# Wide attention: the causal mask written to the scores as four 64x64 tiles instead of two full matmuls

## The reference, cut to what matters

```python
qh = (q @ w_q.T).reshape(b, n, H, D_K).transpose(0, 2, 1, 3)
...
scores = jnp.einsum('bhid,bhjd->bhij', qh, kh) / math.sqrt(D_K)
causal = jnp.tril(jnp.ones((n, n), dtype=bool))
scores = jnp.where(causal[None, None], scores, -jnp.inf)
attn = jax.nn.softmax(scores, axis=-1)
```

## Time and profile before

| | us |
|---|---|
| median of 3 runs | 1951.07 |
| lowest and highest run | 1949.83, 1951.59 |
| profiled execution, its own time | 1948.23 |
| its span, first to last instruction | 1946.2 |
| wide attention in it, first to last mask matmul (L1750) | 353.6 to 800.4 |
| TensorE busy over the whole span | 1779.9 (91%) |
| L1750 within it: 128 matmuls, 379 ns median each | about 33 us of 447 |

### The profile page before, as it was taken

The page is one execution under the profiler, slowest core; times in us unless marked ns, Lnnn a source line. Parts: engine busy times, 40 slices in busy tenths (PEclk is TensorE's granted clock), DMA queues, the critical chain, the costliest instruction groups (busy, mean ns, idle before and its releaser), DMA issues. The chain is left out here.

```text
span 1946.2 us, 43912 instructions
## 1 busy us (share of the span) xinstructions
PE 1779.9 (91%) x16273; PEld 1149.1 (59%) x16273; DVE 1115.4 (57%) x2416; ACT 861.5 (44%) x2151; POOL 613.5 (32%) x1047
## 2 busy tenths in 40 slices
PE   5999878999999999769889999979999989997797
PEld 3555453778778778557763444436777754554343
DVE  4677667566666665561554555552222246776886
ACT  4455425455555555425452333334333344543232
POOL 2667318222222222200103544400000006763440
PEclk9999969999999999869998999978999998999898
DMA  4000040000000000101010000000000010000001
GB/s 108 2 3 3 27 118 6 6 5 7 7 4 7 7 7 2 44 0 44 1 45 1 2 2 2 2 1 0 1 0 0 0 44 2 3 3 2 0 0 43
DMA packets 47708, 27.17 MB, mean 14 GB/s; under 512 B 10928, under 2 KB 44592, under 8 KB 47536
## 3 DMA queue, kind: packets, MB, share of 16 engines
q1 hardware_dynamic: 42800, 24.64, 4.5%
q10 hardware_dynamic: 4736, 0.15, 0.1%
HBM read 22.69 MB, written 2.10 MB: 13 GB/s over the span
## 5 line engine op out<-in xcount | busy, mean ns | idle before, releaser
L708 DVE TENSOR_REDUCE neg_max<-scores 128x8 f32<-128x1024 f32 x192 | 234.8, 1225 | 162.4 <-PE scores L523 66.8
L1708 POOL TENSOR_TENSOR probs<-probs,inverse 128x512 f32<-128x512 f32 x128 | 133.3, 1041 | 337.6 <-DVE inverse L1908 337.6
L651 ACT ACTIVATE probs<-turned 128x1024 f32<-128x1024 f32 x128 | 131.1, 1024 | 224.0 <-PE turned L538 224.0
L493 PE MATMUL scores<-k_diag,q_all 32*128 32x512 f32 x768 | 221.9, 663 | 2.2 <-DVEq L701 2.2
L510 PE MATMUL turned<-q_diag,k_all 32*128 32x512 f32 x768 | 222.0, 653 | 1.1 <-ACT probs L651 1.1
L389 POOL TENSOR_TENSOR k_diag<-k_all,hmask 128x512 f32<-128x512 f32 x96 | 99.8, 1041 | 328.0 <-ACT k_all L630 292.1
L1842 ACT ACTIVATE probs<-scores,neg_max 128x128 f32<-128x128 f32 x512 | 180.7, 387 | 5.3 <-DVE neg_max L1900 5.3
L1409 ACT ACTIVATE hidden_f<-hb_f,b_f 128x512 f32<-128x512 f32 x128 | 88.0, 687 | 130.1 <-PE hb_f L1356 129.9
L1365 PEld LDWEIGHTS yb_f<-w_f,hidden_f 128*128 128x128 f32 x1024 | 119.2, 192 | 14.8 <-issue 14.8
L1365 PE MATMUL yb_f<-w_f,hidden_f 128*128 128x128 f32 x1024 | 119.3, 275 | 0.0
L1356 PE MATMUL hb_f<-xn_all_f,w_f 128*128 (+1 forms) x256 | 118.1, 605 | 0.0
(11 more groups left out here) (292 smaller groups left out, 3675.4 us busy)
## 6 DMA issues: line engine op xcount, KB each, us to landing
ctx_t<-in_ctx_t_dram SPq DMA_DIRECT2D x24, 256.0 KB, 3.2
w_f<-in_L_ffn_W_dram SPq DMA_DIRECT2D x16, 256.0 KB, 3.1
x_state<-in_x_dram SPq DMA_DIRECT2D x4, 512.0 KB, 8.4
ctx_t<-in_ctx_t_dram SPq DMA_DIRECT2D x16, 128.0 KB, 2.1
out_dram<-x_state SPq DMA_DIRECT2D x4, 512.0 KB, 5.4
w_f<-in_L_ffn_We_dram SPq DMA_DIRECT2D x1, 1024.0 KB, 6.8
taps_f<-in_L_ffn_conv_w_dram SPq DMA_DIRECT2D x1, 768.0 KB, 6.4
w_e_f<-_ffn_expert_weights_dram SPq DMA_DIRECT2D x1, 512.0 KB, 4.4
```

The source lines that it names most:

```text
L493: last = nc.tensor.matmul(scores[pair][:, (g % 2) * 512:(g % 2 + 1) * 512], cols(q_all, b, S)[quad_rows(g), :], k_diag[quad_rows(g), b % 2 ...
L651: nc.scalar.activation(probs[:, b % 2, pair, :], turned[:, :], ACT.Exp, **bias).then_inc(s["exp_done"], 1)
L708: v.tensor_reduce(neg_max[:, b % 2, 8 * pair:8 * pair + 8], scores[pair][:, :].rearrange("p (h k) -> p h k", k=S), axis=X_AXIS, op=ALU.max ...
L1708: nc.gpsimd.tensor_tensor(p4, p4, inverse[:, n % 2, CH * h:CH * h + CH].unsqueeze(2).to_broadcast([P, CH, S]), ALU.mult).then_inc(s["prob_ ...
```

## The change

`setup` makes a second table, `causal_swapped`, whose rows 0-63 hold the mask of queries 64-127 and whose rows 64-127 hold that of queries 0-63. `score` then writes the mask of each bank with two matmuls of 64 contracted rows and 64 output partitions. For h = 0 these are rows 0-63 of `causal` to partitions 0-63 and rows 64-127 to 64-127; for h = 1 they are rows 0-63 of `causal_swapped` to partitions 64-127 and rows 64-127 to 0-63. So the four matmuls of an octet use the four different 64x64 quarters of the array. What is computed stays the same.

```diff
--- before.py
+++ after.py
@@ -190,7 +190,7 @@
         def sem(n):
             return nc.alloc_semaphore(n)
         x_in, g_in, zeroed, consts = [sem(f"x_in{c}") for c in range(4)], sem("g_in"), sem("zeroed"), sem("consts")
-        w_zero = sem("w_zero")
+        w_zero, swapped = sem("w_zero"), sem("swapped")
         block = ctx.enter_context(nc.Block())
         chunk = NB // 4
 
@@ -212,6 +212,7 @@
             nc.gpsimd.memset(st.ones[:, :], 1.0)
             nc.gpsimd.memset(st.row0[:, :], 1.0)
             nc.gpsimd.memset(st.causal[:, :], 0.0)
+            nc.gpsimd.memset(st.causal_swapped[:, :], 0.0)
             nc.gpsimd.memset(st.own_rows[:, :, :], 0.0)
             nc.gpsimd.memset(st.ones_pad[:, :], 0.0).then_inc(zeroed, 1)
             pool.wait_ge(zeroed, 1)
@@ -239,7 +240,12 @@
                                     pattern=[[-H, 8], [-1, 4], [-4, 4], [0, DK]], channel_multiplier=1)
             nc.gpsimd.memset(st.v_pad[:, :, :], 0.0)
             nc.gpsimd.memset(st.spread[:, :, :], 0.0)
-            nc.gpsimd.memset(st.ones_b[:, :], 1.0)
+            nc.gpsimd.memset(st.ones_b[:, :], 1.0).then_inc(swapped, 1)
+            for half in range(2):
+                pool.wait_ge(swapped, half + 1)
+                rows = slice(half * 64, half * 64 + 64)
+                nc.gpsimd.affine_select(out=st.causal_swapped[rows, :], in_=st.causal_swapped[rows, :], compare_op=ALU.is_ge,
+                                        fill=NEVER, base=64 - 64 * half, pattern=[[-1, P]], channel_multiplier=1).then_inc(swapped, 1)
 
         @block.scalar
         def _(act):
@@ -1746,10 +1752,11 @@
                 await_kept(pe, place_of(group, "k", 3))
                 await_kept(pe, place_of(group, "q", 3))
                 wait(pe, s["pt_done"], 2 * n - 2)
-                for h in range(2):
-                    nc.tensor.matmul(scores[n % 2][:, h * 512:h * 512 + 512], st.identb[:, :],
-                                     st.causal[:, :].unsqueeze(1).to_broadcast([P, CH, S]), start=True, stop=False,
-                                     skip_group_check=True)
+                for h, table in enumerate((st.causal, st.causal_swapped)):
+                    for r in range(2):
+                        nc.tensor.matmul(scores[n % 2][rows((r + h) % 2), h * 512:h * 512 + 512], st.identb[rows(r), rows(r)],
+                                         table[rows(r), :].unsqueeze(1).to_broadcast([DKW, CH, S]), start=True, stop=False,
+                                         skip_group_check=True)
                 for c in range(CH):
                     for h in range(2):
                         last = nc.tensor.matmul(scores[n % 2][:, h * 512 + c * S:h * 512 + (c + 1) * S],
@@ -2031,7 +2038,7 @@
         st.ln_tmp, st.ln_var = sb("ln_tmp", [P, NB]), sb("ln_var", [P, NB])
         st.ident, st.identb = sb("ident", [P, P]), sb("identb", [P, P], BF16)
         st.ones, st.tri = sb("ones", [P, P]), sb("tri", [P, P])
-        st.row0, st.causal = sb("row0", [P, P], BF16), sb("causal", [P, P], BF16)
+        st.row0, st.causal, st.causal_swapped = (sb(n, [P, P], BF16) for n in ("row0", "causal", "causal_swapped"))
         st.hmask, st.hmask4, st.ident32 = sb("hmask", [P, H]), sb("hmask4", [P, 4]), sb("ident32", [P, 32])
         st.gates, st.tanh_g = sb("gates", [P, 8]), sb("tanh_g", [P, 8])
         st.v_pad, st.ones_pad = sb("v_pad", [P, 2, QUADS * (4 * 32 + DK)]), sb("ones_pad", [P, 32 + 3 * DK])
```

## The result

| | before | after |
|---|---|---|
| median, us (6 runs each) | 1949.44 | 1939.28 |
| lowest and highest run | 1948.63, 1951.59 | 1935.27, 1942.71 |
| profiled execution, its own time | 1948.23 | 1936.97 |
| its span | 1946.2 | 1935.0 |
| wide attention, its first to its last instruction | 477.1 | 469.6 |

The ratio is 0.9946 with a 95% interval of 0.9929 to 0.9962: faster by 0.54%, 10.2 us between the medians. The table already splits the gain: in the profiled executions 7.5 us of 11.2 come from the stage that was changed, and 3.7 us from the rest, in which nothing but the setup differs. Single executions of over 2100 us, which came with and without the change, are left out of all medians and means here.

A forecast was written before the change was run, and what follows sets the result against it. TensorE, full in the wide attention, was taken as the bound. Savings of 46 x 0.06 + 18 x 0.17 = 5.8 us per execution, taken from the median of 1951.07, gave 1945.3 us; the range was 1940 to 1960.

The forecast's parts named there:

- Streams: Mask on TensorE: four matmuls of 512 bf16 columns run together in 0.21 us; 0.85 if none overlap.
- Entry gap: Change of tiling from full-array fill to mask: 0.09 us charged, hidden behind VectorE's copy in masks of the second kind.
- Exit: From mask to the scores' weight load: stream and gap of 0.30 us, as before the change.
- 46 and 18 masks of two kinds: First kind: 46 behind a streaming fill, 0.06 us less each; second: 18, mostly waiting for VectorE's copy, 0.17 less.
- No new wait: Behind the mask: ScalarE's and VectorE's chain starts earlier too; VectorE's slack of 0.17 us exceeds TensorE's lead of 0.06.
- Setup: GpSimd's added memset and two half-height selects cost nothing, covered by SyncE's queue; 1 us without that cover.
- three rounds: Rival: row halves can't write one bank together, two streams (0.43 us) more per mask; 21.7 us slower, 1972.8; chance 0.12.
- two rounds: Rival: mask tiles with the same row half share a read path, one stream (0.21 us) more; 1959; chance 0.08.
- Loads in a row: Rival: the mask's four loads run one after another, 0.24 us in place of 0.08; 4.4 us slower, 1955.5; chance 0.05.
- it does nothing: Rival: TensorE arrives earlier and waits as long at the copy or the heads; 1951; chance 0.05.
- Loads: Mask's weight loads: 0.06 us for a 64-column load plus 0.02 for the fourth tile's later start, 0.08 per mask.
- nothing else moved: Sign of being right: the wide attention gets 5 to 6 us shorter and the rest of the kernel stays the same.

The follow-up runs named there:

- the bank experiment: Changed kernel with the same four mask quarters dealt out so each bank is written by one row half alone; median 1941.41 us, ratio to before 0.9953.
- the two-tile one: Changed kernel with the mask made from the two diagonal 64x64 quarters alone, each used for both banks; median 1952.92 us, ratio to before 1.0018.
- ten variants: The kernel before and nine programs differing from it in the wide attention and its tables alone; time outside that stage and its pause 1467.8 to 1472.4 us.
- the second six runs: The changed kernel run once more with no edit; median 1942.4 us, ratio to before 0.9953.
- Three pauses in the kernel before: Kernel before with GpSimd memsets added at the end of the wide attention, pauses of 2.2, 4.7 and 6.8 us; means 1948.8, 1953.0 and 1954.5 us.

## Why the prediction was wrong in size and right in kind

Right, by its own steps. Streams: four matmuls in one stream's time; taken 0.21, and the scores' load comes 0.33 behind the last start at 513.42 (0.31 in rows 7). Entry gap: 0.09 taken, 0.09 measured. Exit: unchanged. The count of 46 and 18 masks of two kinds held. No new wait, at VectorE's tight place either. Setup: nothing but 0.1 us. The "three rounds" rival, the only one that ended far on the other side, falls with the four starts within 0.01 us and with the bank experiment, "two rounds" with the two-tile one, in which its row pattern is seen and is absent from the change. "Loads in a row" would have had starts 0.06 apart, and "it does nothing" a stage of the old length.

Wrong, first: the term "Loads", 0.06 + 0.02 = 0.08 for one mask. From first load to scores' load are 0.34 us, of which 0.30 is the stream and gap taken over from the earlier trace rows; 0.04 is left for load and stagger. The prediction's lower bound of 0.04, for the load alone, already holds both. The value taken was the fp32 row because it had the right number of columns; the bf16 row had the right type. So a mask of the first kind saved 0.09 where the sum had 0.06, and one of the second 0.18 where it had 0.17 (its loads and stagger took 0.06, as the first matmul started 0.02 behind its load, and its load came 0.01 later): 46 x 0.03 + 18 x 0.01 = 1.6 us, which with rounding is what lies between 5.8 and 7.5. With the stage as measured the forecast would have been 1943.6 from the median then known.

Why the load is that short, and whether it or the stagger is the shorter one, no run here tells.

Wrong, second: "nothing else moved". The sum was carried to the end one for one, with no term for the stages behind. The stage did hand on its 7.5 us, but the rest came out shorter too: 3.7 us between the first two profiles, of which the feed-forward of layer 2, with 10.2 us less at a clock of 0.50, makes 4.8 (the other stages gave 1.1 back). In the means it is 2.5 us, since the kernel before has the longest rest of ten variants, 2.4 us over the mean of the others. 7.1 us from the stage (its two profiles averaged) and 2.5 from the rest make the 9.6 us between the means.

Wrong, third: the starting point. The number forecast was counted from a median of three runs, 1951.07, and with six it is 1949.44. So the 6.0 us between 1945.3 and 1939.28 are 1.6 of starting point, 1.7 of loads and 2.7 of what is not the stage.

The range was one-sided: it reached 15 us up for rivals and 5 down, and had no term for the clock of untouched stages, whose spread within one kernel (1934.7 to 1943.3 over 12 runs) is larger than the gain that was forecast. On which side of 1940 the median fell was chance as well: that of the second six runs, 1942.4, lies inside the range.

Open: what sets the rest. Three pauses in the kernel before gave 1469.5, 1471.2 and 1470.6 in place of 1472.4, and only the first is clear of the noise by itself. That it can come out this short without the change is shown. That the moment at which the later stages start is the cause is only argued: a pause also leaves TensorE idle for longer, which the change does not do, and two executions whose feed-forward began at the same moment had different clocks in it. No run gives a rule by which to forecast it.

## What to carry to other kernels

Count a switch of the array's tiling as a term of its own: 0.09 us of gap, and the loads behind it stand in the open. Four 64x64 quarters at once pay only if they are four different ones, and pay most if the neighbours in the order have the same tiling, so that no switch is left between them (here 13 us more, on top of the 7.5 of the change). And where a change is worth a few us in one stage, read that stage's length in profiles of both kernels; the total has the clock of all other stages in it. A median of six runs can fall between two groups, so compare means of a dozen or more.

## What the runs showed of the hardware that was not expected

A load of 64 bf16 columns with 64 rows leaves at most 0.04 us before its stream can run, stagger of four tiles included, where the fp32 load of 64 columns took 0.06. Starts of the mask's matmuls in 64x64 tiles lie 0.003 to 0.004 us apart (four within 0.01), those of 32-row tiles 0.007 (rows 7, four within 0.02). It is not the tile's size alone: the four score tiles of 64x64 start within 0.01 in the kernel with both mask and scores tiled (0.28 us for four records of 0.27) and within 0.02 behind a full mask (0.34 for four of 0.32). A pause of 2.2 us at the end of a stage cost a kernel of 1949 us nothing that could be measured. In the layer 2 feed-forward, one and the same stream of work had its clock at 0.50 for 10.2 us in some executions and for none in others.
